# Cross-attention on one core: key weights folded into the queries, and the context's split parts kept in DRAM

## What is computed

```python
qh = (q_in @ wq + bq).reshape(b, q_len, H, K)
kh = (kv_in @ wk + bk).reshape(b, t, H, K)
vh = (kv_in @ wv + bv).reshape(b, t, H, K)
kh = jnp.concatenate([kh, jnp.broadcast_to(bias_k, (b, 1, H, K))], axis=1)
...
logits = jnp.einsum('bqhk,bthk->bhqt', qh, kh) / scale
weights = jax.nn.softmax(logits, axis=-1)
ctx = jnp.einsum('bhqt,bthk->bqhk', weights, vh).reshape(b, q_len, H * K)
return ctx @ wo + bo
```

## Time and profile before

| | us |
|---|---|
| median of 3 runs | 2243.7 |
| the runs | 2246.68, 2243.7, 2242.16 |
| span of the profiled execution | 2244.8 |
| PE busy | 2160.7 (96%) |
| DVE busy | 1558.1 (69%) |
| ACT busy | 1247.0 (56%) |
| POOL busy | 822.3 (37%) |
| mean granted TensorE clock | 0.989 |

### The profile page before, as it was taken

One profiled execution on the slowest core, in us unless ns is written; L12 is line 12 of the kernel. 1 busy time (PEld: TensorE's weight loads), 2 busy tenths in 40 slices (PEclk: granted clock), 3 DMA queues, 4 the chain that ended last, 5 costly groups with the idle time before them and its releaser, 6 DMA issues.

```text
span 2244.8 us, 36949 instructions
## 1 busy us (share of the span) xinstructions
PE 2160.7 (96%) x12468; PEld 2097.8 (93%) x12468; DVE 1558.1 (69%) x3631; ACT 1247.0 (56%) x2956; POOL 822.3 (37%) x754
## 2 busy tenths in 40 slices
PE   7999999999999999999999999999999989898999
PEld 6999999999999999999999999998999878786999
DVE  7777788777778877776887777787445577678241
ACT  5555555555555555554655555556366476567464
POOL 4314444241344424234442423442556311022355
PEclk9999999999999999999999999999999999899999
DMA  4657445565745555464555546454453756755243
GB/s 139 168 138 179 99 116 102 123 150 138 179 101 113 103 124 125 83 151 95 119 102 126 123 85 150 101 113 74 126 166 112 188 144 175 206 149 134 70 124 112
DMA packets 161447, 287.77 MB, mean 128 GB/s; under 512 B 35312, under 2 KB 92784, under 8 KB 161264
## 3 DMA queue, kind: packets, MB, share of 16 engines
q1 hardware_dynamic: 161264, 285.41, 53.1%
HBM read 240.32 MB, written 28.64 MB: 120 GB/s over the span
## 4 chain that ended last, share of the span: by engine, by line
PE 82%; DVE 4%; ACT 4%; DMA 4%; issue 2%; POOL 2%; SPq 1%; ACTq 0%; POOLq 0%; DVEq 0%
PE bank L873 77%; PE bank L966 3%; DMA k<-k_parts 2%; DMA ctxN_raw<-in_ctx 2%; POOL mring L808 1%; ACT prob L1389 1%; PE bank L1146 1%; DVE prob L1722 1%; DMA stage<-in_fb 1%; PE bank L1135 1%; DVE ln_c L1607 1%; SPq L676 0%; DVE qs L1554 0%; DVE ctxT L1558 0%; POOL mring L806 0%
## 5 line engine op out<-in xcount | busy, mean ns | idle before, releaser
L873 PE MATMUL bank<-ctxT,kring 128*128 128x362 f32 x3456 | 632.0, 330 | 6.6 <-DVE kT L1554 5.5
L873 PEld LDWEIGHTS bank<-ctxT,kring 128*128 128x128 f32 x3456 | 589.2, 190 | 9.6 <-POOL mring L808 6.1
L808 POOL TENSOR_TENSOR mring<-stage,mring 128x512 fp32r<-128x512 f32 x325 | 443.9, 1372 | 165.3 <-ACT mring L1275 148.1
L873 PE MATMUL bank<-pT,ctxN 128*128 128x400 f32 (+1 forms) x2304 | 471.2, 352 | 0.3 <-DVE U L1558 0.3
L806 POOL TENSOR_SCALAR mring<-stage 128x512 fp32r<-128x512 f32 x205 | 143.5, 700 | 856.8 <-PE bank L873 712.8
L873 PEld LDWEIGHTS bank<-pT,ctxN 128*128 128x128 f32 (+1 forms) x2304 | 408.7, 189 | 1.8 <-issue 0.6
L873 PE MATMUL bank<-hT,mring 128*128 128x400 f32 x1608 | 320.1, 348 | 7.7 <-POOL mring L808 4.5
L873 PE MATMUL bank<-U,mring 128*128 128x400 f32 x1536 | 303.3, 348 | 8.1 <-issue 6.4
L873 PEld LDWEIGHTS bank<-hT,mring 128*128 128x128 f32 x1608 | 294.9, 189 | 14.1 <-POOL mring L808 7.3
L873 PEld LDWEIGHTS bank<-U,mring 128*128 128x128 f32 x1536 | 275.3, 188 | 10.3 <-issue 7.9
L1275 ACT ACTIVATE kT<-bank,cols 128x361 fp32r<-128x361 f32 (+1 forms) x288 | 160.7, 558 | 211.3 <-PE bank L873 211.2
(11 more groups left out here) (103 smaller groups left out, 2954.1 us busy)
## 6 DMA issues: line engine op xcount, KB each, us to landing
ctxN_raw<-in_ctx SPq DMA_DIRECT2D x256, 192.0 KB, 3.7
ctxT_raw<-in_ctx SPq DMA_DIRECT2D x64, 724.0 KB, 7.8
k<-k_parts SPq DMA_DIRECT2D x96, 181.0 KB, 3.7
stage<-in_wk SPq DMA_DIRECT2D x64, 256.0 KB, 4.9
stage<-in_wq SPq DMA_DIRECT2D x64, 256.0 KB, 4.6
stage<-in_wv SPq DMA_DIRECT2D x64, 256.0 KB, 4.1
stage<-in_wo SPq DMA_DIRECT2D x64, 256.0 KB, 2.7
stage<-in_fa SPq DMA_DIRECT2D x64, 256.0 KB, 2.6
```

Of the source, the lines that this page charges most:

```text
L808: nc.gpsimd.tensor_tensor(lo, src, f32(hi), ALU.subtract).then_inc(S.w_ready, 1)
L873: mm = pe.matmul(dst, parts_l[a], parts_r[b], start=first and k == 0, stop=last and k == len(order) - 1)
```

## The change

L0's attentions are rebuilt; L1 and the MLPs keep their shapes (some buffers move).

- **Fold.** Keys are no longer computed. `fold` multiplies each head's query by the key weights: four chunks c, each 3 products of 400 columns into a bank of its own, each read by ScalarE and VectorE into `QU`. Logits are then `QU` times the transposed context, 512 deep: 12 products of 362 columns.
- **Packing.** Heads come in groups of 5, 5 and 6: 12 groups (8 of five, 4 of six). For a batch, five heads are 500 rows, cut into 4 tiles of 125 rows; six are 600 rows, 5 tiles of 120. There are 208 logits tiles; before there were 256 of 100 rows. `value_sums` has 500 columns once, or 300 columns twice.
- **The learned row.** Its logit comes from `extra_logits` (products of 4 columns, 32 or 40 for a group), is selected by three VectorE operations (`extra_select`) and put into column 1 of each logits bank by `put_extra`.
- **Order.** A group is now a phase of projections (`queries`, `fold`, and `values` and `project` of the group before, in turns, through three banks) and then a phase of tiles (one logits tile, one turn, the value sums, in each step).
- **Context.** It is split in groups 0 and 3 alone, and saved in DRAM (`c_parts`, `n_parts`); the other ten groups load both parts, twice the bytes.
- **`p0_row`** is 600 columns wide and has one buffer.

```diff
-GN = 16
-LAG = 3
+GROUP_HEADS = [5, 5, 6]
+TILE_ROWS = {5: 125, 6: 120}
+NG = 12
+LAG = 2
...
+def sum_step(G, b, c, k):
+    n = tiles_of(G)
+    return n * (b + 1) + LAG + (c if n == 4 else [0, 0, 1, 1, 2, 2, 3, 4][2 * c + k])
...
-        p0_row = sb("p0_row", [1, 2, ROWS], F32)
+        p0_row = sb("p0_row", [1, BROWS], F32)
...
+            def proj_bank_free(key):
+                n = PROJ_AT[key]
+                if n >= 3:
+                    pe.wait_ge(S.proj_done, n - 2)
...
+            def fold(G, h):
+                key = ("k", G, h)
+                tile_ready(key)
+                pe.wait_ge(S.proj_done, PROJ_AT["q", G, h, 0] + 1)
+                for c in range(DC):
+                    proj_bank_free(("k", G, h, c))
+                    split_mms(proj_bank(("k", G, h, c)), w_cols(key, c), [q_head(p_, h) for p_ in range(2)],
+                              True, True).then_inc(S.proj_mm, 1)
...
+                pe.wait_ge(S.e_put, n + 1)
+                first, last = tile_columns(G, b, j)
+                for c in range(DC):
+                    mm = split_mms(bank[2 + n % 2][0:tile_rows(G), 2:LT + 2], [QU[:, p_, c, first:last] for p_ in range(2)],
+                                   ctxT_c(i, c), c == 0, c == DC - 1)
...
+            def turned_high(n):
+                G, b, j = TILES[n]
+                act.wait_ge(S.t_mm, n + 1)
+                high(turned_to(G, b, j, 0), turned_from(n)).then_inc(S.pt_hi, 1)
+                if j == 0 and NB * G + b:
+                    before = NB * G + b - 1
+                    act.wait_ge(S.p0_in[before % NB], 16 * (before // NB + 1))
+                size = tile_rows(G)
+                high(p0_row[0:1, j * size:(j + 1) * size], bank[T_BANK[n % 2]][0:1, 0:size]).then_inc(S.p0_copied, 1)
```

More of the change, by code:

```diff
@@ new lines, in projections @@
+def projections(G):
+    now, before = heads(G), heads(G - 1)
+    items = []
+    if now:
+        items.append(("q", G, 0))
+    if before:
+        items.append(("v", G - 1, 0))
+    for s in range(max(now, before)):
+        if s + 1 < now:
+            items.append(("q", G, s + 1))
+        if s < now:
+            items.append(("k", G, s))
+        if s == now - 1:
+            items.append(("e", G, 0))
+        if s + 1 < before:
+            items.append(("v", G - 1, s + 1))
+        if s < before:
+            items.append(("o", G - 1, s))
+    return items
@@ new lines @@
+PROJ = [projections(G) for G in range(NG + 1)]
+PROJ_OUT = []
+for items_ in PROJ:
+    for kind_, G_, h_ in items_:
+        if kind_ in "qv":
+            PROJ_OUT.append((kind_, G_, h_, 0))
+        elif kind_ == "k":
+            PROJ_OUT += [(kind_, G_, h_, c_) for c_ in range(DC)]
+PROJ_AT = {key: n for n, key in enumerate(PROJ_OUT)}
+PROJ_HIGH = list(itertools.accumulate(key[0] != "v" for key in PROJ_OUT))
+HEAD_AT = {("v", G, h): sum(heads(g) for g in range(G)) + h for G in range(NG) for h in range(heads(G))}
@@ new lines, in extra_logits @@
+            def extra_logits(G):
+                pe.wait_ge(S.extra_ready, 4)
+                pe.wait_ge(S.proj_done, PROJ_AT["q", G, heads(G) - 1, 0] + 1)
+                layer, n = stage_of(G)[1], tiles_of(G)
+                for b in range(NB):
+                    for j in range(n):
+                        first, last = tile_columns(G, b, j)
+                        h = first_head(G) + j
+                        at = 4 * (b * n + j)
+                        for p_ in range(2):
+                            mm = pe.matmul(bank[E_BANK][0:tile_rows(G), at:at + 4], qT[:, p_, first:last],
+                                           extra_k[:, layer, h:h + 2, :].rearrange("p h k -> p (h k)"),
+                                           start=p_ == 0, stop=p_ == 1)
+                mm.then_inc(S.e_mm, 1)
@@ new lines, in values, with project @@
+                mm.then_inc(S.proj_mm, 1)
+            def project(G, h):
+                key = ("o", G, h)
+                tile_ready(key)
+                last = h == heads(G) - 1
+                pe.wait_ge(S.v_lo, HEAD_AT["v", G, h] + 1)
+                if h == 0:
+                    pe.wait_ge(S.pt_lo, last_tile(G))
+                for c in range(DC):
+                    mm = split_mms(bank[O_BANK[c]][:, 0:ROWS], w_cols(key, c), two(v_parts[:, v_slot(G, h)]),
+                                   h == 0, last)
+                    if last and c < DC - 1:
+                        mm.then_inc(S.oc_mm, 1)
```

1087 lines of the change are left out of this document (563 added, 524 removed).

## The result

| | before | after |
|---|---|---|
| median | 2244.3 us | 2636.0 us |
| runs | 2242.2 to 2246.7 (4) | 2634.1 to 2638.1 (4) |
| profiled execution's span | 2244.8 | 2634.6 |
| PE busy | 96% | 86% |
| mean granted TensorE clock | 0.989 | 0.921 |

The changed kernel is slower: the ratio is 1.174 (95% interval 1.172 to 1.176), 392 us more, where 180 was forecast. The sign and the main term held; the size did not, and the time lies outside the range. Nearly all of the loss is in L0's attentions: from the last value-sum product to the end are 662.3 us before and 669.0 after.

The account below looks back on a forecast made before the run. TensorE's issue was taken as the limit. Work -55, edges -8 and -6, fold +35, tiles +13, groups 0 and 3 +31, `p0_row` wait +142, clock +28: +180 on 2244.8, less 1.1, 2424 us; range 2310 to 2500.

Parts of the forecast that it names:

- The sign: Whole kernel: slower than before by more than about 0.2%, chance 0.91.
- main term: ACT's wait for the landing of the single `p0_row`'s DMA, passed on to PE: +142 us.
- What bounds: Before the change, TensorE's issue is the limit: PE busy 1426 of 1439 us, so each added wait is paid.
- step 6: One `p0_row`: ACT waits for the previous batch's DMA, landing in 10.8 or 12.5 us, and PE stalls: +142 us.
- Rival B: Landing of the `p0_row` DMA does not grow with bytes and stays 9.1 us: +90, 2334 us, chance 0.08.
- C: The `p0_row` landing wait is absorbed, landing below 5.3 us, only the work left: -27, 2217 us, chance 0.07.
- Step 7: PE's slower clock behind the landing stalls, 1.7 us for each long one: +28 us (0 to 40).
- rival D: Small products cost 0.19 us each (+51) and the DMA queue saturates, loads late (+25): 2500 us, chance 0.09.
- Step 5: Groups 0 and 3: all context splits on ACT and DVE, plus saves in the loads' queue: +31 us (0 to 40).
- Step 1: Work of PE: 1546 us before, 1491 after, small products at 0.067 each: -55 us.
- Steps 3 and 4: Fold products wait for banks, +35 us (10 to 55); projection reads and learned-row operations precede first logits, +13 (0 to 25).
- Step 2: Edges of stages: half the extra behind normalisations goes, -8 us; shorter tail and no keys needed at the start, -6.

Follow-up runs that it names:

- the second edit: Changed kernel with the spread of the learned row issued behind the step's loads in each group's last batch: 2563.2 us.
- the best form: Changed kernel without the landing wait, 128 partitions kept, fourth chunk's load before the last spread, early saves, four projection banks for three: 2306.8 us, ratio 1.027 to the kernel before.

## Why the prediction was right or wrong

**What bounds, and step 6: right.** The wait was placed, and sized, where the trace has it: stalls of 8.4, 6.5, 7.2 for 8.58, 7.24, 7.24; 2.5, 0.7, 2.5 for 3.5, 1.4, 1.4; none at the fourth batch. The landing grew with the bytes, to 11.2 and 12.9, for 10.8 and 12.5 of "204.8 kB / 30 = 6.8 us and 2.3 fixed"; the estimate from the port rate of the Trainium skill ("SBUF — State Buffer", section "Door 1: The DMA port swizzle (why `[64,N]` ≈ `[32,N]`)") gave 11.0 and 12.9 and was closer. In the groups of five the near size is in part luck: they stop at the turn and not at the sum, and the three stops are off by up to 1.1 each way. Rival B is out, and C with it. Step 7's 1.7 for a long stop (its row gives 6.72 - 5.13 = 1.6) measured 2.1 behind the first. Steps 6 and 7 together were +170; taking the wait away gives 178.5. A part of that is the splitting groups, which stop for 8.9 + 7.2 + 7.7 in place of 6.3; without ACT's wait PE's waits for the split `ctxT` fall from 32.4 to 16.2.

**The failed step: a load behind the spread.** Step 6 counts the landing only as a wait of ACT; that the same spread holds back the load issued behind it stands at nothing in the sum. The prediction named it in rival D as "the queue saturates" with +25, from the queue's mean load, 15.8 of 17.2 us. It is not a mean. In each group's last batch a load stands directly behind 11 us of spread and is wanted after 9: 73 by the second edit alone. Which transfer is late could have been read from the order of SP's program.

**Step 5: wrong in mechanism and size.** "Splits were spread evenly over 16 groups; now all is in two": +31 for the splits on ACT and DVE and for crowding. The two groups are 31 and 35 longer than group 9, 65, and early saves take away 68. What was not seen is the wait of SP itself, for a save to land before a load to the same place.

**Step 1: the price of small products.** It took 0.067 from the transposes, and "the transposes' period disagrees" with the P/1.2 ns of the Trainium skill ("TensorE: Matmul & The Clock Gate", section "LDWEIGHTS (loading the stationary operand)"). That row was misread. The three transposes of the earlier trace rows start at 191.71, 191.80 and 191.89, 0.09 apart, and only the product behind them follows after 0.03, at 191.92; 0.067 is the mean of unlike distances. The small products agree with the Trainium skill: 0.099 at full clock, for an estimated 0.104 with its P of 125. That is 0.032 x 416 = +13, and the slower clock behind a clump, in no step, another 16 net of the longer wait. (The run without 382 of them says 19 over the forecast for both, also net.) The rest of the step could be seen in the trace: a step of five heads is 1258.64 - 1254.29 = 4.35 for 4.30, 10 in all, so by these two the work shrank by some 32, not 55.

**Steps 3 and 4: about right.** In group 7 the fold's idle times are 0.28 + 0.49 for the first head and 0.26 plus short ones for each other, some 3.7 a group by the distances from the first product of each fold to the next block, 44 for 35; four banks gave back 22 and 17 (with the clump of small products back in the latter). Waits ahead of the logits are 13.0 in 12 groups, as forecast, though step 4's own items (0.69 and 0.24) add up to 11.

**Step 2.** The start gained nothing that the trace shows. The first query comes at 19.4 instead of 28.8, but the first logits at 58 instead of 34, since a phase of five heads stands between, and in the first 60 us PE is busy 42.7 at a granted clock of 0.85, for 45.9 at 0.97 before. Neither this nor the +4.1 behind a normalisation was tested.

**The sum.** +180 forecast. The wait and the order of the load together measured 237.5 where steps 6 and 7 had 170, + 68; with + 34 for the saves, + 29 for the small products and + 9 for the fold that is 320 of 392. The other 72 have no experiment of their own; the best form shows what they can be. It stands 62 over the kernel before, where the terms of the work, edges, fold and first logits sum to -21, so 83 are missing, and about 20 more if the fold's term is lowered by what four banks gave back. Its trace has 8.7 of waits for `ctxN` and 6.9 for `ctxT`, and its two splitting groups stop for 5.3 + 3.9 + 3.3 + 2.2 besides. Small products cost 13 more and their clock 16, steps are 0.05 longer (208 x 0.05 = 10), and what comes behind the last value sum is 5 longer. That makes some 75, with the small products' two terms taken over from above; the rest, 8 to some 30, stays open.

## What to carry over

When a wait for a DMA's landing is added, read what stands next in the order of issue as well as on the engines: here a slow transfer delayed the load issued just behind it, and in the phase where steps are short that load was late. A save that frees a place must be issued early enough to land before the next load to it is due. And an experiment that removes a wait should leave the transfer's shape alone: one row fewer, 127 for 128, moved the result by 89 us.

## What the hardware showed

- A broadcast from one partition to 128 lands at a median of 9.1 us for 400 columns and 11.2 for 500, and at 12.9 for 600: 51.2 kB more take 1.7 to 2.1 us, 24 to 30 GB/s. The longest landing in any of the 128-row runs is 13.6.
- A 384-KB load issued 1.3 us behind such a broadcast landed in 10.7 us from the same queue and in 10.8 from another engine's; the one issued just ahead of it took 4.0.
- The same DMA to 127 partitions ran at a DMA share of 0.06 and 23 to 25 GB/s, to 128 at 0.81 and 30. Behind the first a load in the same queue took 15.3, and 5.7 when the broadcast was in another queue. The median of all `ctxN` loads was 10.9 with 127 rows and 7.4 with 128.
- 32 products of 4 columns in a row, at full clock, were followed by a stretch granted 0.58; behind 8 in a row, ahead of further products, it stayed 1.00.
